# A three-layer field-interaction kernel: fewer fields in pairs, another order of chunks, norms and gathers

## What is computed

```python
e = stack([tbl_f[ids[:, f]] for f in range(39)], axis=1)          # 512 x 39 x 16
prev = e
for k in range(3):                                                # w0: 39*39 x 128; w1, w2: 39*128 x 128
    z = einsum('bmd,bhd->bdmh', e, prev).reshape(b, D, m * h)
    t = transpose(einsum('bdc,co->bdo', z, ws[k]) + bs[k], (0, 2, 1))
    t = t / sqrt(sum(t * t, axis=(-2, -1), keepdims=True))
    logit.append(t)
    prev = t
h = concatenate([sum(concatenate(logit, axis=1), axis=-1), dense_ctx], axis=1)
y = relu(relu(h @ W_top1 + b_top1) @ W_top2 + b_top2) @ W_top3
```

## Time and profile before

| | |
|---|---|
| median of 3 runs | 1323.89 us (1323.67 to 1325.28) |
| the profiled execution | 1321.28 us, span 1319.4 us |
| TensorE busy | 1170.5 us, 89% of the span |
| VectorE busy | 984.2 us, 75% |
| GpSimd busy | 912.1 us, 69% |
| ScalarE busy | 113.7 us, 9% |
| mean granted clock of TensorE | 0.962 of full speed |
| HBM traffic | 155 GB/s over the span |

### The profile page before, as it was taken

The page is one execution under the profiler, slowest core; times in us unless marked ns, Lnnn a source line. Parts: engine busy times, 40 slices in busy tenths (PEclk is TensorE's granted clock), DMA queues, the critical chain, the costliest instruction groups (busy, mean ns, idle before and its releaser), DMA issues.

```text
span 1319.4 us, 21655 instructions
## 1 busy us (share of the span) xinstructions
PE 1170.5 (89%) x7868; PEld 581.0 (44%) x7868; DVE 984.2 (75%) x836; ACT 113.7 (9%) x219; POOL 912.1 (69%) x614
## 2 busy tenths in 40 slices
PE   0888989999898998979899897999989799898989
PEld 0334545444444444435344453544445354444443
DVE  2596878788587878858788686878868687887771
ACT  0010100101000010100101000010101001010102
POOL 5565877777676786767678586777858677655660
PEclk9889989999899999989999999998999999899989
DMA  6946265463635645364463626546362654537010
GB/s 174 389 123 252 59 223 150 145 205 98 212 85 181 191 135 185 89 205 131 145 212 105 226 58 222 150 145 201 104 236 60 203 168 145 193 101 245 1 42 1
DMA packets 104409, 204.31 MB, mean 155 GB/s; under 512 B 49131, under 2 KB 52075, under 8 KB 104390
## 3 DMA queue, kind: packets, MB, share of 16 engines
q1 hardware_dynamic: 97610, 202.52, 46.8%
q0 software_dynamic: 5120, 1.29, 1.0%
q10 hardware_dynamic: 1660, 0.25, 0.1%
HBM read 201.72 MB, written 2.30 MB: 155 GB/s over the span
## 4 chain that ended last, share of the span: by engine, by line
issue 29%; POOL 29%; PE 27%; DVE 7%; DMA 2%; SPq 2%; POOLq 1%; ACT 1%; DVEq 0%; ACTq 0%
POOL sums L278 12%; PE acc L690 9%; POOL gathered L243 9%; PE mix_ps L690 8%; PE acc L676 8%; POOL sums L281 6%; DVE z L543 4%; DMA w_sb<-in_w 2%; POOL rows_of L237 1%; SPq L351 1%; ACT cross L442 1%; PE t_ps L782 1%; DVE inv L589 0%; DVE u L552 0%; DVE v L556 0%
## 5 line engine op out<-in xcount | busy, mean ns | idle before, releaser
L543 DVE TENSOR_TENSOR z<-t_ps,xb 128x2048 f32<-128x2048 f32 (+1 forms) x352 | 708.2, 2042 | 100.3 <-PE acc L690 79.8
L281 POOL TENSOR_TENSOR sums<-z,sums 128x1024 f32<-128x1024 f32 x192 | 454.5, 2367 | 15.1
L278 POOL TENSOR_TENSOR sums<-z 128x512 f32<-128x512 f32 x192 | 250.6, 1305 | 285.2 <-DVE z L543 276.9
L676 PE MATMUL acc<-z,w_sb 128*64 128x512 f32 x1920 | 434.3, 596 | 7.4 <-DVE z L543 7.4
L690 PE MATMUL mix_ps<-sums,s_sb 128*64 128x256 f32 x1536 | 299.3, 391 | 28.8 <-POOL sums L281 25.8
L690 PE MATMUL acc<-z,w_sb 128*64 128x256 f32 x768 | 244.9, 402 | 78.8 <-DVE z L543 78.8
L676 PEld LDWEIGHTS acc<-z,w_sb 128*64 128x64 f32 x1920 | 138.2, 138 | 243.0 <-issue 229.3
L690 PE MATMUL mix_ps<-z,w_sb 128*64 128x256 f32 x768 | 244.8, 402 | 0.0
L690 PE MATMUL acc<-z,s_sb 128*64 128x256 f32 x768 | 243.0, 400 | 0.0
L690 PE MATMUL p_ps<-z,w_sb 128*64 128x256 f32 x768 | 243.0, 400 | 0.0
L243 POOL DMA_INDIRECT gathered<-in_table,rows_of x160 | 180.5, 1128 | 65.8 <-issue 48.3
(11 more groups left out here) (73 smaller groups left out, 413.8 us busy)
## 6 DMA issues: line engine op xcount, KB each, us to landing
xb<-xt SPq DMA_DIRECT2D x80, 768.0 KB, 5.8
xb<-xq SPq DMA_DIRECT2D x96, 512.0 KB, 4.5
xb<-xt SPq DMA_DIRECT2D x96, 512.0 KB, 5.7
xr<-xt SPq DMA_DIRECT2D x144, 156.0 KB
x<-xt SPq DMA_DIRECT2D x45, 78.0 KB
gathered<-in_table,rows_of POOLq DMA_INDIRECT x160, 4.1
xr<-xt SPq DMA_DIRECT2D x32, 78.0 KB
xt<-gathered SPq DMA_DIRECT2D x16, 72.0 KB, 2.3
```

The source lines that it names most:

```text
L278: nc.gpsimd.tensor_tensor(t2, t3, b11, ALU.add).then_inc(sums_ready, 1)
L281: nc.gpsimd.tensor_tensor(t41, b2, t2_twice, ALU.subtract).then_inc(sums_ready, 1)
L543: nc.vector.tensor_tensor(z[:, at:at + n, :], t_ps[k - 1][:, :].rearrange("p (a n) -> p a n", a=1).broadcast_to([P, n, N]), xb[:, XB_ROW[c ...
L676: last = nc.tensor.matmul(acc[k][o, :], w_sb[k][:, D_FIELD + 3 * d + r, o], z[:, at + r, :], start=(c == 0 and r == 0), stop=(c == NCH - 1 ...
```

## The change

`PAIR_GROUPS` goes from 3 to 2: eight pairs (16 fields) in four P chunks, and 23 plain fields in seven D chunks, of three or four fields each. The order is now D3 D3 P P D4 D3 P P D4 D3 D3, set by the list `PLAIN_IN`. In either case there are 11 chunks, of 39 rows together. The rest moves operations: on VectorE the norm sums, the norm, the scaling and the end of layer 2; on TensorE the norm's matmul, from behind (2,4) to behind (2,6); on GpSimd three of the ten gathers, from layer 1's end to layer 2's end.

```diff
-PAIR_GROUPS = 3
+PAIR_GROUPS = 2
-CHUNKS = [("D", 0), ("P", 0), ("P", 1), ("D", 1), ("P", 2), ("P", 3), ("D", 2), ("P", 4), ("P", 5), ("D", 3), ("D", 4)]
+PLAIN_IN = [3, 3, 0, 0, 4, 3, 0, 0, 4, 3, 3]
+
+def chunks():
+    out, field, p = [], PAIRED, 0
+    for n in PLAIN_IN:
+        out.append(("D", field, n) if n else ("P", p, 4))
+        field, p = field + n, p + (not n)
+    return out
...
-                            gather(i + 2, range(0, 8))
+                            gather(i + 2, range(0, 5))
                         if k == 2 and c == LAST_P and gathers:
-                            gather(i + 2, range(8, GROUPS))
+                            gather(i + 2, range(5, GROUPS))
...
-            sp.wait_ge(z_ready, chunks_to(TILES - 1, 2, 1))
+            sp.wait_ge(z_ready, chunks_to(TILES - 1, 2, 2))
...
                 for c in range(NCH):
                     products(i, 1, c)
-                    if c == 0 and not first:
+                    if c == 1 and not first:
                         shared_sums(i - 1, 2)
-                    if c == 1 and not first:
+                    if c == 2 and not first:
                         add_shared(i - 1, 2)
...
                     products(i, 2, c)
-                    if c == 1:
+                    if c == 3:
                         norm_sums(1, i)
-                    if c == 2 and not last:
+                    if c == 4 and not last:
                         norm_sums(0, i + 1)
-                    if c == 4:
+                    if c == 9:
                         normalize(i + 1, *layers_of(first, last))
-                    if c == 5 and not last:
-                        scale0(i + 1)
+                        if not last:
+                            scale0(i + 1)
...
-                for r in range(3):
+                for r in range(n):
...
-                layer(i, 2, range(0, 5), first)
+                layer(i, 2, range(0, 7), first)
                 add_partitions(i + 1, *layers_of(first, last))
-                layer(i, 2, range(5, NCH), first)
+                layer(i, 2, range(7, NCH), first)
```

More of the change, by code:

```diff
@@ L38 @@
 LOADS0 = [(0, 2), (2, 4), (4, 6), (6, 7)]
-PAIR_GROUPS = 3
+PAIR_GROUPS = 2
 PAIRED = 2 * GROUP * PAIR_GROUPS
 PAIRS = PAIRED // 2
-CHUNKS = [("D", 0), ("P", 0), ("P", 1), ("D", 1), ("P", 2), ("P", 3), ("D", 2), ("P", 4), ("P", 5), ("D", 3), ("D", 4)]
+PLAIN_IN = [3, 3, 0, 0, 4, 3, 0, 0, 4, 3, 3]
[5 more added lines that the diff above has]
+    return out
+CHUNKS = chunks()
 NCH = len(CHUNKS)
[L56 to L59, removed]
+XB_ROW = [sum(n for _, _, n in CHUNKS[:c]) for c in range(NCH + 1)]
+FIRST_P = PLAIN_IN.index(0)
+LAST_P = NCH - 1 - PLAIN_IN[::-1].index(0)
 NP = PAIRS // 2
 STEPS = 2 * NCH
-D_FIELD = PAIRED
 RING = 14
@@ L70, in ring @@
     for s in range(STEPS):
-        n = ROWS_OF[CHUNKS[s % NCH][0]]
+        n = CHUNKS[s % NCH][2]
         if pos + n > RING:
@@ L77, in ring @@
     for s in range(STEPS):
-        n = ROWS_OF[CHUNKS[s % NCH][0]]
+        n = CHUNKS[s % NCH][2]
         for d in range(1, STEPS + 1):
             r = (s - d) % STEPS
-            if at[r] < at[s] + n and at[s] < at[r] + ROWS_OF[CHUNKS[r % NCH][0]]:
+            if at[r] < at[s] + n and at[s] < at[r] + CHUNKS[r % NCH][2]:
                 back.append(d)
@@ L354, in load_chunk @@
             def load_chunk(i, c):
-                t, d = CHUNKS[c]
+                t, d, rows = CHUNKS[c]
                 plain = xt[bass.ds(i, 1), :, :].rearrange("a m n -> (a m) n")
@@ L358, in load_chunk @@
                 if t == "D":
-                    load_rows(c, plain, D_FIELD + 3 * d, 3, XB_ROW[c])
+                    load_rows(c, plain, d, rows, XB_ROW[c])
                 else:
@@ L532, in products @@
                 s = (k - 1) * NCH + c
-                at, n = RING_AT[s], ROWS_OF[CHUNKS[c][0]]
+                (kind, _, n), at = CHUNKS[c], RING_AT[s]
                 if c == 0:
@@ L536, in products @@
                 if k == 1:
-                    dve.wait_ge(xb_loaded[c], (16 if n == 3 else 32) * (i + 1))
+                    dve.wait_ge(xb_loaded[c], (16 if kind == "D" else 32) * (i + 1))
                 back = RING_BACK[s]
@@ L671, in direct @@
             def direct(i, k, c):
-                d = CHUNKS[c][1]
+                _, field, n = CHUNKS[c]
                 at = RING_AT[(k - 1) * NCH + c]
-                for r in range(3):
+                for r in range(n):
                     for o in (LEFT, RIGHT):
-                        last = nc.tensor.matmul(acc[k][o, :], w_sb[k][:, D_FIELD + 3 * d + r, o], z[:, at + r, :],
-                                                start=(c == 0 and r == 0), stop=(c == NCH - 1 and r == 2),
+                        last = nc.tensor.matmul(acc[k][o, :], w_sb[k][:, field + r, o], z[:, at + r, :],
+                                                start=(c == 0 and r == 0), stop=(c == NCH - 1 and r == n - 1),
                                                 skip_group_check=True)
```

## The result

The changed kernel takes 1234.32 us (median of 4 runs, 1234.13 to 1234.45), the kernel before 1323.78 beside it: a ratio of 0.9324, 95% interval 0.9307 to 0.934. The forecast was 1235. The span fell from 1319.4 to 1232.3 us, by 87.1 where the sum had 90.

What follows compares the result with a forecast made beforehand. TensorE, stalled because VectorE waits for ScalarE's root, bounds the kernel; a tile of 70.1 work plus 2.0 waits replaces 77.8, so span 1230 + 1.9 + 2.6 = 1235 us, range 1222 to 1247.

Steps and rivals of the forecast that it cites:

- the sum: Whole run: steady tile 77.8 to 72.1 us, 14 times; first and last 4.8 less each; span 1319.4 to 1230.
- The wait for the root: VectorE's reciprocal waits 7.24 us for ScalarE's root; moving the norms removes it and TensorE's 4.62 stall and 2.88 slow chunk.
- the forecast's price: Four fields a layer go from pairs to plain: 0.84 us a layer, 1.7 us a tile more on TensorE.
- The work: TensorE's work in a steady tile: 68.4 us before, 70.1 with the added plain fields.
- The new waits: TensorE waits for GpSimd's second sums in layer 1: 0.5 us at chunk 2, 1.5 at chunk 3, together 2.0 a tile.
- The walk: Step-by-step timing from TensorE's end of layer 2's chunk 6 to next tile's layer 1, chunk 3; finds 2.0 us of waits.
- The clock: TensorE keeps full speed after the new waits; mean clock above 0.98.
- The half-clock rival: After the new waits, 4 us at 0.58 lose 1.7 us a tile: +24, 1259 us; chance 0.14.
- The gathers: GpSimd's gathers go 5+5 for 8+2; behind layer 2's chunk 7 they land at 12 us, before the mixing needs them.
- the 8 us in hand: GpSimd's slack between gathers landing at 12 us and the mixing, which waits for all ten, at 19.7.
- the late sums of (2,1): Layer 2, chunk 1: the old block of eight gathers sometimes delayed its sums, as at 330.74; that source goes.

Runs made afterwards that it cites:

- The norm alone: Kernel before with only the norm's matmul, norm operations and scaling moved later, twelve pairs and old gathers kept: 1240.43 us, ratio 0.9368.
- the chunks alone: Changed kernel with norms, layer end and gathers put back, keeping only eight pairs, 23 plain fields and their order: 1335.62 us, ratio 1.0086.
- Moving the mixing: Changed kernel with GpSimd's mixing of rows moved from behind the sums of layer 1's chunk 2 to behind those of chunk 3: 1222.48 us, ratio 0.9236.
- moving the head: Changed kernel with layer 2's shared sums and its end each moved one chunk later in the next tile's layer 1: 1204.16 us, ratio 0.9088.
- 8 and 2: Changed kernel with the gathers back at eight behind layer 1 and two behind layer 2: 1235.03 us, ratio 0.9324.
- norm in the gap: Changed kernel with norm matmul behind layer 2's chunk 5, norm and scaling behind chunk 7's products, where VectorE idles: 1226.95 us, ratio 0.9261.
- The kernels of twelve pairs: Norm-alone kernel with later shared sums, layer end and mixing, gathers 5 and 5: 1193.98 us; with two norm scratch tiles also in PSUM: 1184.83 us.

## Why the prediction was right

**The bound and what releases it.** Right. The wait for the root is gone, TensorE's waits for VectorE went from 78.8 to 4.3 us in its pair chunks, the mean clock from 0.962 to 0.993. The norm alone brings 84 us, the chunks alone lose 11. Together they bring 90 and not 73: the kernel with the norm alone has two losses that the whole change has not, the held operation (19 us) and the long tiles (12 us), and is spared the plain fields (16 x 1.7 = 27 us by the forecast's price); 1240 - 31 + 27 is 1236, for 1234 measured.

**The work.** 23 plain fields were to make 70.1 us a tile; 72.34 less the two waits of 2.07 is 70.27.

**The new waits.** The walk gave 0.5 and 1.5, together 2.0; the trace has 0.89 and 1.18, together 2.07. The place, the order of those late and the sum are right, the split is not. The first was under-sized by 0.4: VectorE and GpSimd took about 0.2 more, handovers among it (sums ready 636.94 - 617.07 = 19.87 us after the start of (2,8), for 19.69), and TensorE came about 0.2 sooner (wanting them at 636.11, 19.04 after it, for 19.23). The second is smaller since the larger first had moved TensorE further, and the mixing takes 0.76 in place of 0.86, its tiles being narrower. That the two slips cancel in the sum is luck. Moving the mixing, and moving the head, each took away what the walk says.

**The clock.** Right: 1.00 over both stretches of the earlier trace rows's kind in the tile shown, 0.993 in the mean. The half-clock rival did not come: behind both waits the clock was 1.00 in all 15 tiles that have them. The argument from the earlier trace rows was weak, though. The pair of waits before 331, 0.82 and 1.77 us, was followed by 0.58; almost the same pair in the kernel with the norm alone, 0.86 and 1.77 us, was followed by 1.00 over 316.86 to 320.86. What decides it stays open.

**The gathers.** Right in the outcome: 8 and 2 against 5 and 5 makes no difference, and none of the mixings in the loop waits for them. But the forecast had one reading wrong. It took the 3.4 us before a gather in the earlier trace rows for a single wait for TensorE. The kernel before has three more such pauses, of 4.37, 2.31 and 2.15 us, for which the profile names no releaser, and every kernel here has four of over 2 us in its loop. In the changed kernel three of the four fell into the block behind (2,7), the longest with 5.26 us, and the 8 us in hand took them up. The forecast also put the late sums of (2,1) down to the block of eight; with eight pairs that block came back (8 and 2) and no tile was long, so it is rather the room around it that changed. In that kernel the pauses were only 2.2 us, so it is no full test.

**The sum.** -5.7 a tile against 77.80 - 72.34 = 5.46 measured, 14 times 0.2 being the 3 us between the 90 and the 87.1 of the span.

What the forecast did not say, because it did not have to: that the change keeps something that costs. It priced the plain fields at 1.7 us a tile but gave no rival in which they were not needed. The kernels of twelve pairs are 40 and 49 us faster than the change; 30 of these the later head gives to eight pairs as well, so the pairs themselves are worth 10 to 19 us. And in two of the expectations for the experiments (norm alone, norm in the gap) the same term was missing: VectorE's small operations were costed at their duration beside idle or gathering GpSimd.

## What to carry to other kernels

Where one engine is to run ahead of another through a ring of buffers, put what it must wait for where the ring would stop it anyway; the gain is the bubble and the slow clock behind it. Then walk the chain from the ring's last release to the next use, step by step from start-to-start times, and move out of it what is wanted later: here two lines moved by one chunk were worth another 30 us. Before giving up cheap arithmetic to relieve an engine, try the order first, and look at single stages as well as the mean: an engine that keeps up in most of them may still be late behind a rare pause.

## What the runs showed of the hardware

- A VectorE operation of 128 x 96 with both inputs in SBUF took 2.32 us beside a GpSimd addition of 128 x 1024 and ended with it; with one input in PSUM it took 0.27 at the same place. Beside GpSimd's gathers it took 0.26.
- Two gather issues beside VectorE products of two SBUF tiles took 1.96 us (at 658.33 in the changed kernel) and 2.75 us (at 631.71 in the kernel before), for a median of 0.94. One that began 0.03 us before such a product (at 657.09) took 0.94.
- Between two gathers GpSimd stood for 2.1 to 5.5 us four times in the loop of each kernel, for the usual 0.30. No trace here shows why.
- The other way round, GpSimd's row numbers (128 x 10) took 1.18 us in the kernel before, where VectorE was multiplying two SBUF tiles, and 0.21 in the changed kernel, where it was not. The two first products for layer 0, which read two SBUF tiles, went from 3.08 us to 2.35, now that no sum runs beside them. I had costed both at the old durations; they lie where there is slack.
- Waits of 0.89 and 1.18 us with 3.5 us of work between them left TensorE's granted clock at 1.00 (2.4 GHz), tile after tile; one of 4.09 us was followed by 0.57 over four microseconds. A pair of 0.8 and 1.8 us, 2.4 us apart, was followed by 0.58 in one kernel and by 1.00 in another.
